# One transformer layer on one core: straight engine programs, the second norm folded into the Gelu's scale, no quantiser, centred second weights

## What is computed

```python
xn = (x - mean) / sqrt(var + 1e-5)
x  = x + attn(xn) + ffn(xn)

def attn(x):                      # 16 heads of 16, causal window of 64 plus 4 sink columns
    q = x @ Wq.T; latent = x @ Wkv_down.T
    k = latent @ Wk_up.T; v = latent @ Wv_up.T
    return softmax(mask(q k^T / 4)) v @ Wo.T

def bitlinear(x, w):              # used twice, w_fc (1024 x 256) and w_proj (256 x 1024)
    xn = (x - mean) / sqrt(var + 1e-6)
    g = max|xn|;  x_hat = clip(xn * 128 / g, -128 + 1e-6, 128 - 1e-6) * g / 128
    gam = mean|w|; w_hat = sign(round(w / (gam + 1e-6))) * gam
    return x_hat @ w_hat.T

def ffn(x): return bitlinear(gelu(bitlinear(x, w_fc)), w_proj)
```

## Time and profile before

| | us |
|---|---|
| median of three runs | 197.97 |
| lowest and highest run | 197.04, 198.84 |
| span of the profiled execution (first to last instruction) | 195.3 |
| TensorE busy | 160.2 (82%) |
| VectorE busy | 148.7 (76%) |
| ScalarE busy | 104.3 (53%) |
| GpSimd busy | 81.9 (42%) |
| mean granted TensorE clock | 0.877 |

### The profile page before, as it was taken

How to read it: one execution, slowest core, us unless ns; L and a number is a source line. 1 busy time by engine, 2 the same in 40 slices (tenths; PEclk the granted TensorE clock), 3 DMA queues, 4 the chain that set the end, 5 groups by cost and what they waited for, 6 DMA issues and landing times.

```text
span 195.3 us, 4915 instructions
## 1 busy us (share of the span) xinstructions
PE 160.2 (82%) x1954; PEld 106.9 (55%) x1954; DVE 148.7 (76%) x261; ACT 104.3 (53%) x152; POOL 81.9 (42%) x106
## 2 busy tenths in 40 slices
PE   1827947789978499999969499999799999997953
PEld 1515512445865466556756456647667764676731
DVE  0689999996999976655999976678997877696341
ACT  2557601356999222076997122368994314899020
POOL 6240192003089800450199601430598215059830
PEclk9999955579999755899999756999999999999975
DMA  6995000001000000013000000030000002100001
GB/s 170 334 330 168 3 2 0 3 18 38 3 3 2 0 3 0 3 54 109 0 0 0 0 0 0 0 106 5 0 0 7 0 3 65 43 3 3 0 3 54
DMA packets 7836, 7.49 MB, mean 38 GB/s; under 512 B 2500, under 2 KB 7464, under 8 KB 7720
## 3 DMA queue, kind: packets, MB, share of 16 engines
q1 hardware_dynamic: 6108, 6.02, 10.2%
q10 hardware_dynamic: 1712, 1.25, 2.1%
HBM read 6.21 MB, written 1.05 MB: 37 GB/s over the span
## 4 chain that ended last, share of the span: by engine, by line
PE 51%; DVE 26%; ACT 10%; issue 8%; DMA 2%; POOL 1%; DVEq 0%; ACTq 0%; SPq 0%
PE ring L1003 7%; PE acc L1161 7%; PE ring L1028 5%; PE ring L1122 4%; PE aux L1239 3%; PE ring L1033 3%; DVE xn L734 3%; ACT E L473 3%; PE ring L1150 3%; DVE t2s L810 3%; PE ring L1216 3%; DVE gh L803 2%; ACT EH L474 2%; PE aux L1178 2%; DVE sth L785 2%
## 5 line engine op out<-in xcount | busy, mean ns | idle before, releaser
L351 POOL TENSOR_TENSOR EL<-E,EH 128x1024 f16<-128x1024 f32 x16 | 36.3, 2296 | 37.4 <-ACT EH L474 28.4
L713 DVE TENSOR_REDUCE mx<-ring 128x4 f32<-128x768 f32 x16 | 14.7, 951 | 6.3 <-PE ring L1033 6.3
L474 ACT ACTIVATE EH<-ring,un 128x1024 f16<-128x1024 f32 x16 | 17.8, 1115 | 0.0
L473 ACT ACTIVATE E<-ring,un 128x1024 f32<-128x1024 f32 x16 | 17.8, 1112 | 0.0
L1028 PE MATMUL ring<-mask,idb 128*128 128x384 bf16 (+1 forms) x48 | 14.7, 393 | 2.2 <-DVE vs L890 2.2
L1150 PE MATMUL ring<-idf,t2s 128*128 128x128 f32 x64 | 10.4, 316 | 5.8 <-DVE Q L851 5.2
L399 POOL TENSOR_SCALAR ve<-mv 128x2 f32<-128x2 f32 x4 | 1.0, 239 | 32.5 <-DVE gx L757 32.4
L487 ACT ACTIVATE gl<-ring,a 128x1024 f32<-128x1024 f32 x8 | 8.9, 1116 | 9.1 <-PE ring L1003 9.1
L1161 PE MATMUL acc<-prT,t2h 128*128 128x256 f16 x48 | 13.2, 311 | 0.0
L1122 PE MATMUL ring<-xhT,wqT 128*128 128x256 f16 x64 | 11.1, 302 | 2.5 <-ACT EH L474 2.5
L1161 PE MATMUL acc<-prT,t2l 128*128 128x256 f16 x48 | 13.1, 309 | 0.0
(11 more groups left out here) (220 smaller groups left out, 464.7 us busy)
## 6 DMA issues: line engine op xcount, KB each, us to landing
wfc_r<-in_L_ffn_w_fc SPq DMA_DIRECT2D x1, 1024.0 KB, 7.3
wpr_r<-in_L_ffn_w_proj SPq DMA_DIRECT2D x1, 1024.0 KB, 9.6
xres<-in_L_attn_x SPq DMA_DIRECT2D x4, 256.0 KB, 2.8
out<-ob SPq DMA_DIRECT2D x4, 256.0 KB, 2.2
bias<-in_c_bias SPq DMA_DIRECT2D x1, 825.0 KB
xin<-in_L_attn_x ACTq DMA_DIRECT2D x3, 256.0 KB, 2.6
wq_r<-in_L_attn_Wq ACTq DMA_DIRECT2D x1, 256.0 KB, 3.3
xin<-in_L_attn_x SPq DMA_DIRECT2D x1, 256.0 KB, 3.9
```

The source lines that it names most:

```text
L351: nc.gpsimd.tensor_tensor(EL[at].rearrange("p g t q -> p g (t q)"), E32[:, r], EH[at].rearrange("p g t q -> p g (t q)"), ALU.subtract).the ...
L473: nc.scalar.activation(E32[:, r], src[:], ACT.Exp, scale=un[:, 0:1]).then_inc(ex[0], 1)
L474: nc.scalar.activation(EH[at].rearrange("p g t q -> p g (t q)"), src[:], ACT.Exp, scale=un[:, 0:1]).then_inc(exh[0], 1)
L713: nc.vector.tensor_reduce(out=o, in_=src[:, :, 0:2 * (T - BLK)].rearrange("p a (t k) -> p a t k", t=2), axis=AX.X, op=ALU.max).then_inc(re ...
```

## The change

All engine programs are written out for the four batches, with no loop and with constants in every wait, and each engine has an order of its own, as a list of calls. The ring's order is built as one list (`ORDER`), with other neighbours than before.

The arithmetic is changed in three places. First, the quantiser goes: no `cx`, `gx`, `txs`, `thT`, `tlT` in the rows, no `ch`, `gh` (as maximum), `t2s` in the hidden layer. The first feed-forward product reads `xhT` and `xlT`, the halves that q reads too. Second, the second norm of the rows is only a factor: GpSimd works it out from the first norm's variance, and with `gam` it becomes `a1`, the scale in the Gelu. Third, the hidden mean isn't subtracted from `gl`; instead each row of the second ternary weight is centred. TensorE transposes `gl` itself, and ScalarE and VectorE write its halves (`gh`, `glo`) times `gam_r`. Mean and variance of `gl` are still taken, for `a2` alone.

```diff
-                        nc.vector.tensor_reduce(out=gx[:, i:i + 1], in_=cx[:, i, :], axis=AX.X, op=ALU.max,
-                            nc.vector.tensor_scalar(txs[:, i, :], cx[:, i, :], gxq[:, i:i + 1], None, ALU.mult).then_inc(tx_ok[0], 1)
-                    nc.vector.tensor_tensor(tlT[:], src[:, 1, :].rearrange("p (c t) -> p c t", c=CC), thT[:], ALU.subtract).then_inc(tl_ok[0], 1)
...
+            def row_factors(n):
+                nc.gpsimd.tensor_tensor(vr[:], mv1[:, :, 1], rs1[:], ALU.mult).then_inc(row2[0], 1)
+                nc.gpsimd.tensor_tensor(vn[:], vr[:], rs1[:], ALU.mult).then_inc(row2[0], 1)
+                nc.gpsimd.tensor_scalar(ve2[:], vn[:], FFN_EPS, None, ALU.add).then_inc(row2[0], 1)
+                nc.gpsimd.tensor_tensor(rs2[:, n % 2, :], ve2[:], neghalf[:, 0:TT_], ALU.pow).then_inc(row2[0], 1)
...
+            def first_scale(f):
+                nc.gpsimd.tensor_scalar(a1[:], rs2[:, f % 2, :], gam[:, 0:1], None, ALU.mult).then_inc(a1_ok[0], 1)
...
+            def hidden_high(b, i):
+                nc.scalar.activation(gh[:, i].rearrange("p k n -> p (k n)"), flat(slot("t2T", b, i)),
+                                     ACT.Copy, scale=gam_r[:, 0:1]).then_inc(gh_ok[0], 1)
...
-                    nc.vector.tensor_scalar(ch[:, i, :], gl[:, i, :], mvh[:, i, 0:1], None, ALU.subtract).then_inc(ch_ok[0], 1)
-                    nc.vector.tensor_reduce(out=gh[:, i:i + 1], in_=ch[:, i, :], axis=AX.X, op=ALU.max,
-                    nc.vector.tensor_scalar(t2s[:, i, :], ch[:, i, :], ghr[:, i:i + 1], QB, ALU.mult, ALU.mult).then_inc(t2[0], 1)
+                nc.vector.scalar_tensor_tensor(out=glo[:, i].rearrange("p k n -> p (k n)"), in0=flat(slot("t2T", b, i)), scalar=gam_r[:, 0:1],
+                                               in1=gh[:, i].rearrange("p k n -> p (k n)"), op0=ALU.mult, op1=ALU.subtract).then_inc(glo_ok[0], 1)
...
+            def second_ternary():
+                for c in range(CC):
+                    did_pro(nc.vector.scalar_tensor_tensor(out=neg_t[:, 0, c * F:(c + 1) * F], in0=wpr_r[:, c, :], scalar=pthr[:, 1:2],
+                                                           in1=neg_t[:, 1, c * F:(c + 1) * F], op0=ALU.is_gt, op1=ALU.subtract,
+                                                           accum_out=tsum[:, c:c + 1]))
+                did_pro(nc.vector.tensor_scalar(tmean[:], tsum[:], 1.0 / F, None, ALU.mult))
+                for c in range(CC):
+                    nc.vector.tensor_scalar(tern[:, 1, c * F:(c + 1) * F], neg_t[:, 0, c * F:(c + 1) * F], tmean[:, c:c + 1], None,
+                                            ALU.subtract).then_inc(w_tern, 1)
...
+                hidden_transposed(b, 0)
+                hidden_transposed(b, 1)
+                window_scores(b, 0)
+                window_scores(b, 1)
+                if more:
+                    latents(b + 1)
+                second_product(b, 0)
+                window_scores(b, 2)
+                second_product(b, 1)
+                window_scores(b, 3)
+                if more:
+                    q_products(b + 1)
+                    k_products(b + 1)
+                values_high(b)
+                if more:
+                    v_products(b + 1)
+                values_low(b)
```

More of the change, by code:

```diff
@@ L281, in hidden_slot, with back_first @@
[L281 to L297 removed]
+        def back_first(b):
+            return ([("fc", b, i, [(gelu, b, i + 1)]) for i in range(TT_)])
@@ L615, in _ @@
         @block.vector
         def _(dve):
-            def flat(t):
-                return t.rearrange("p a n -> p (a n)")
             pro = [0]
@@ L955, in _ @@
-            last.then_inc(w_tr, 1)
-            pe.wait_ge(w_sq, 5)
-            nc.tensor.matmul(acc[:, 0:10], ones[:], flat(wsq), start=True, stop=True).then_inc(w_sqtot, 1)
             N_EV, N_LO = 6, 10
@@ L1060, in latents, with q_products @@
+            def q_products(f):
+                if f == 0:
+                    pe.wait_ge(w_lo, 6)
+                s = take("f_q", f)
+                for t in range(NT):
                     for n, (x_half, w_half) in enumerate(HALVES):
                         for c in range(CC):
-                            last = nc.tensor.matmul(aux[:, 0:T], wkvT[:, w_half, c].rearrange("p d l -> p (d l)"), (xhT, xlT)[x_half][:, c, :],
-                                                    start=(n == 0 and c == 0), stop=(n == 2 and c == CC - 1))
@@ new lines, in q_products, with k_products @@
+                last.then_inc(mm_q[0], 1)
+            def k_products(f):
+                wait(pe, lath_ok, f)
+                wait(pe, latl_ok, f)
+                if f == 0:
+                    pe.wait_ge(w_lo, N_LO)
+                s = take("f_k", f)
+                for t in range(NT):
+                    for w_half, deep in STACKED:
+                        last = nc.tensor.matmul(s[:, t // 2, (t % 2) * T:(t % 2 + 1) * T],
+                                                wkT[0:deep, w_half, G * t:G * t + G].rearrange("p h d e -> p (h d e)"), lat[0:deep],
+                                                start=(w_half == 0), stop=(w_half == 1), skip_group_check=True)
+                last.then_inc(mm_k[0], 1)
@@ new lines, in sink_maxima @@
+            def sink_maxima(f, o):
+                wait(pe, bd_ok, f)
+                nc.tensor.matmul(o[:, 0:H * SINK], idb[:], msink[:], start=True, stop=False, skip_group_check=True)
+                for i in range(TT_):
+                    for t in range(NT):
+                        last = nc.tensor.matmul(o[:, i * H * SINK:(i + 1) * H * SINK], Q[:, t, i * P:(i + 1) * P], BDH[:, t, 0:H * SINK],
+                                                start=False, stop=(t == NT - 1), skip_group_check=True)
+                return last
@@ new lines, in fc_tile @@
+            def fc_tile(b, i):
+                if b == 0:
+                    pe.wait_ge(w_ev, N_EV + 2)
+                s = take("fc", b, i)
+                for n in range(2):
+                    for m, (c, src) in enumerate([(c, src) for src in (xhT, xlT) for c in range(CC)]):
+                        last = nc.tensor.matmul(s[:, n, :], src[:, c, i * P:(i + 1) * P], fcT[:, c, 512 * n:512 * n + 512],
+                                                start=(m == 0), stop=(m == 2 * CC - 1))
+                last.then_inc(fc[0], 1)
@@ new lines, in hidden_transposed, with second_product @@
+            def hidden_transposed(b, i):
+                s = take("t2T", b, i)
+                wait(pe, gelu, b, i + 1)
+                for k in range(FC):
+                    last = nc.tensor.transpose(s[:, k // 4, (k % 4) * P:(k % 4 + 1) * P], gl[:, i, k * P:(k + 1) * P], idf[:])
+                last.then_inc(tr_h[0], 1)
+            def second_product(b, i):
+                wait(pe, glo_ok, b, i + 1)
+                if i == 0:
+                    wait(pe, y_ok, b - 1)
+                    if b == 0:
+                        pe.wait_ge(w_ev, N_EV + 4)
+                for k in range(FC):
+                    for src in (gh, glo):
+                        last = nc.tensor.matmul(acc[:, i * C:(i + 1) * C], src[:, i, k, :], prT[:, k, :],
+                                                start=(i == 0 and k == 0 and src is gh), stop=(k == FC - 1 and src is glo), skip_group_check=True)
+                last.then_inc(pr[0], 1)
```

1362 lines of the change are left out of this document (592 added, 770 removed).

## The result

The changed kernel takes **203.23 us** (median of four, 201.89 to 205.68) against 198.28 us for the kernel before (four, 197.04 to 198.84) on the same chip: a ratio of **1.022, interval 1.015 to 1.028**. It is slower where 187 us and faster were forecast. The profiled execution spans 200.1 us.

What follows compares the result with a forecast made beforehand. VectorE's chain makes TensorE wait in the loop passes, and half clock doubles the price. Passes -7.6, -6.8, +0.2, last pass +2.7, prologue +0.7: -10.8, so span 195.3 to 184.5; with 2.7 added, 187 us, range 181 to 194.

Steps and rivals of the forecast that it cites:

- so I take it to stay at 1.00: First three passes: TensorE's granted clock stays at 1.00, since no single wait there exceeds 0.8 us.
- 35.2: Each of the first three passes, at full clock, takes 35.2 us instead of 42.8, 42.0 and 35.0.
- its own waits of about 1.6: Third pass before the change: TensorE's waits of about 1.6 us, subtracted from 35.0 in a second derivation.
- wait 0.5: End of each pass: TensorE waits 0.5 us while VectorE normalises until 29.55.
- plus 2.7: Last pass: 34.2 us, 2.7 more, as values wait for all exponentials and TensorE then runs at half clock.
- plus 0.7: Prologue: 44.7 us, 0.7 more, between -1 and +4, with centring of the second ternary weight added.
- The loop's removal at 0: Loop's branch: writing out the loop gains 0, since TensorE shows no stop there.
- Rival (c): Passes: TensorE falls to 1.2 GHz once in each, costing 3.6 us four times; 202 us, chance 0.05.
- (a): Passes: TensorE's work alone bounds them at 33.6 us, small waits vanish, last pass at full clock; 181 us, chance 0.10.
- (b): Values: GpSimd's low halves become the bound, with a chain 2.5 us longer than counted; 194 us, chance 0.12.
- (d): Loop passes: VectorE's removed chain wasn't the limit, only the clock gains; 194 us, or 197 with 2 more, chance 0.07.
- Span to median, 2.7: Whole kernel: the median of the runs lies 2.7 us above the profiled span.

Runs made afterwards that it cites:

- e5: Changed kernel's arithmetic in straight code, but with the engine orders of the kernel before: 184.93 us against 197.47 for the kernel before.
- e10: Changed kernel with two `VH` buffers, last pass in old orders, and eight discarded 512-column matmuls per pass between values high and v: 196.11 us.
- e2: Changed kernel plus eight discarded 512-column matmuls between values high and v in each of three passes: 205.94 us, ratio 1.041.
- e9: Changed kernel with two `VH` buffers and its last pass alone in the old orders: 196.13 us.
- e3: Changed kernel plus ten discarded 512-column matmuls in the wait ahead of each pass's latent product: 209.52 us.
- e7: New arithmetic in the old orders, with one group of eight hidden transposes moved from behind values high to ahead of it: 195.06 us, ratio 0.989.
- e12: The changed kernel run once more, unaltered, for the spread of its profile: 205.42 us.
- e14: New arithmetic, old orders, both hidden transposes ahead of values high, plus 13 discarded 32-row, 192-column matmuls between values high and low: 202.16 us.
- e1: Kernel before with only its loop over three passes written out: 197.11 us against 197.07, ratio 0.998.
- e13: New arithmetic, old orders, both hidden transposes ahead of values high, plus five discarded 128-row, 512-column matmuls between values high and low: 194.81 us.
- e6: Changed kernel with the next batch's first two rounds of maxima moved between values high and v, nothing added: 213.79 us.

## Why the prediction was wrong

- **The step that failed: "so I take it to stay at 1.00".** It was inferred from idle time alone: no wait of the walk was longer than 0.8 us, and the clock had survived one such wait. The waits came out as walked (0.64, 0.73, 0.51 and 0.43 us), but the long falls came with TensorE's busy share at 1.00, in the run of k, values high, v and values low that the new order had put together. The same arithmetic in the old orders (e5) had 0.95, 1.00 and 0.95 where this one had 0.79, 0.87 and 0.76. The waits are not cleared either: the fall at 133.6 us stood behind two of them and lasted 3.4 us, which is some 1.4 us at the price above. The three passes are 123.3 us long, 17.7 above three times 35.2. The profiled span is 15.6 above the forecast's 184.5, so this step is all of the miss and more (the last pass added 0.7, the prologue of this profile gave back 2.8).
- **The passes' length at full clock, 35.2,** is borne out, as far as it can be read: 35.0 by the line, 35.1 or less in e10 with two buffers. In the second derivation of it "its own waits of about 1.6" is misread: the third pass before was idle for 1.40 us (35.00 less 33.60, rows 2), which makes 35.4. The walk of TensorE's work held within 0.2 us to values low.
- **"wait 0.5"** for the normalised `y` was mis-derived. The walk let `VH` be written when v was ready and missed that one buffer, still read by values low, holds it. The transposes came 1.75 us later than walked. The wait itself was 0.51 us, right by accident: at half clock the work ahead of it lasted longer. At full clock it would have been 1.80, as in e2, and a pass up to 1.3 us longer than walked.
- **The last pass, "plus 2.7"**: it measured 34.9 against 34.2, so plus 3.4, with the stop of 3.7 us ahead of the values and the half clock as walked. e9 shows the old order worth 4.5 us there.
- **The prologue, "plus 0.7", 44.7 us.** The first profile has 41.9, but eight more profiles have this very prologue (e2, e3, e5 to e7, e12 to e14), and there it took 43.8 to 45.75, with a mean of 44.7. The size was right and the first profile an outlier. The second ternary weight took 3.6 us (36.37 to 39.97 on VectorE) against 2.33 in the earlier trace rows: 1.3 more, taken as 1.5.
- **The loop's removal at 0**: right, by e1. By the rule of the Trainium skill ("Runtime: NRT & Kernel Launch", "Instruction fetch mechanics") a gain was possible; the ratio of 0.998 shows none that can be measured.
- **Rival (c)** had the time nearly right (202), at a chance of 0.05. Its price of 3.6 us per pass was too low (the three passes lost 5.9 each against the forecast), and its trigger was wrong for the long falls: it waited for an idle stretch. That the time came out is in part luck. Its argument "the fall came only behind the wait of 2.60" did not hold in the trace of before either. In the first loop pass the clock fell at 65.5 us, 0.3 us into such a wait, and the stretch ahead, with values high in it, was nearly full (the lines stand below). Had I asked of each pass what stands next to what, the order itself would have shown that the hidden transposes left the values' neighbourhood, which the third pass before, at clock 1.00, had them in.

```profile
62.50:65.50 3.00, 2.71 (x101) 1.00 0.00 0
...
67.80 1.94 PE L1150 MATMUL ring<-idf,t2s 128*128 128x128 f32 x8 [2.59 <-DVE Q L851]
```

- The Trainium skill, "TensorE: Matmul & The Clock Gate", Part 1, which I had cited for the throttled state as the default, was read with idle time in mind. The runs show falls without any: the granted clock went to 0.50 by 110 us with a busy share of 1.00.
- **Rivals (a), (b), (d)**: GpSimd's low halves (2128 ns each) were never waited for in the changed kernel's passes (b); e5 shows the gain with VectorE's chain gone, so (d) is out (its 194 with 2 us more is 196, not 197); (a) needed the clock.
- **Span to median, 2.7**: a profiled run stands 1.8 us above its own span (201.89 against 200.1 here, 185.09 against 183.3 in e5). The other 0.9 of the 2.7 was scatter of the runs, not what lies around the instructions.

## What to carry to other kernels

When an order moves dense matmuls away from thin ones, check the granted clock before counting waits: a busy share of 1.00 does not vouch for it. Where independent dense work can stand between products of few columns, try it there before moving it earlier. Here 1.25 us of dense matmuls in that gap of each of three passes, against as much time of thin ones, was worth 7 us; against an empty gap it only paid for itself, so it is worth having where the dense work is needed anyway. When a producer is pulled ahead of the last reader of its old value, list its buffers first.

## What the runs showed of the hardware

- TensorE was granted 1.2 GHz with a busy share of 1.00 throughout (109 to 111 us of the first profile), and stayed there for 3.4 to 20.5 us.
- In the gap of e13 and e14, 1.25 us of matmuls with 128 rows and 512 columns left two whole passes of the profiled run at clock 1.00; 1.27 us of 32-row, 192-column ones left them at 0.87 and 0.91. Over the whole kernel the clock was 0.885 to 0.937 against 0.846 to 0.862 in four runs each.
- Falls stood behind waits too: 2.83 us of waiting in the first pass of e7, e13 and e14 was followed by one each time. A wait of 1.06 us was followed by one in e7 but not in e13 and e14, where the second pass has the same wait.
- A microsecond at half clock cost 0.38 to 0.42 us in these passes, not 0.5: part of the low time lies over waits, and small matmuls gain less from the clock (32 of 17 columns took 0.68 us at full clock in e2 and 1.03 at half in the changed kernel).
- The falls come at different places from execution to execution of the same kernel, and the times scatter with them: 203.8 to 217.5 us in e6, 196.5 to 199.9 for the kernel before.
